# Edge rows of every third tile added on Pool instead of VectorE, in a graph-attention layer on one core

## The reference

```python
h = jnp.maximum(_layernorm(x, axis=-1), 0.0)          # x: 50000 x 256
msg = jax.nn.relu(h[src] + edge_attr)                 # 25000 edges, 256 wide
p = msg @ W_fc.T + b_fc
scores = p @ Q.T                                      # 4 heads
...
alpha = w / jnp.maximum(denom[dst], 1e-09)            # softmax over the edges of a node
pooled = segment_sum(alpha[:, h:h+1] * p, dst)        # for each head
gate = softmax(mean_p @ Wg.T + bg)                    # mean_p: mean of p over a node's edges
return x + sigmoid(einsum('nh,nht->nt', gate, pooled))
```

## Time and profile before

| | us |
|---|---|
| median of 3 runs | 658.44 |
| lowest, highest | 654.64, 659.47 |
| profiled execution, first to last instruction (the profile gives no other time of it) | 732.9 |
| VectorE busy in it | 487.6 |
| Pool busy in it | 453.4 |
| TensorE busy in it | 548.9 |

### The profile page before, as it was taken

The page is one execution under the profiler, slowest core; times in us unless marked ns, Lnnn a source line. Parts: engine busy times, 40 slices in busy tenths (PEclk is TensorE's granted clock), DMA queues, the critical chain, the costliest instruction groups (busy, mean ns, idle before and its releaser), DMA issues.

```text
span 732.9 us, 12416 instructions
## 1 busy us (share of the span) xinstructions
PE 548.9 (75%) x2474; PEld 434.1 (59%) x2475; DVE 487.6 (67%) x1644; ACT 383.3 (52%) x661; POOL 453.4 (62%) x339
## 2 busy tenths in 40 slices
PE   2417988878779868879403998888888778877785
PEld 2205876666558656758202876776667566665564
DVE  4208678788879768769798766666565655555555
ACT  2105455656457545647211254666666666666674
POOL 7765565665560656550053366777877887778785
PEclk9999899999999999989855999999999999999999
DMA  7434455555553468775300799999999999999999
GB/s 223 131 93 134 147 173 174 165 174 154 174 170 114 129 224 271 237 234 191 115 0 1 247 355 383 314 307 329 357 319 329 325 327 339 325 337 336 341 333 332
DMA packets 137238, 171.53 MB, mean 234 GB/s; under 512 B 10096, under 2 KB 123784, under 8 KB 137202
## 3 DMA queue, kind: packets, MB, share of 16 engines
q10 hardware_dynamic: 91344, 90.23, 37.6%
q1 hardware_dynamic: 33010, 42.70, 18.6%
q0 software_dynamic: 12848, 38.20, 16.5%
HBM read 111.50 MB, written 59.60 MB: 233 GB/s over the span
## 4 chain that ended last, share of the span: by engine, by line
PE 52%; issue 12%; ACT 11%; DVE 10%; another core or an unknown queue 5%; ACTq 4%; DVEq 3%; POOL 2%; DMA 2%; POOLq 0%; SPq 0%
PE bank L745 24%; PE bank L829 18%; PE bank L735 7%; ACT arena L597 5%; DVE spread L1248 3%; ACT bank L573 3%; POOL arena L478 2%; ACTq L600 2%; DVEq L1252 1%; ACT arena L505 1%; ACTq L552 1%; ACTq L605 1%; ACT arena L497 1%; DMA p_keep<-p_spill 1%
## 5 line engine op out<-in xcount | busy, mean ns | idle before, releaser
L829 PE MATMUL bank<-p_keep,spread 128*128 x1172 | 274.1, 388 | 51.6 <-DVE spread L1248 46.7
L829 PEld LDWEIGHTS bank<-p_keep,spread 128*128 128x128 f32 x1172 | 219.0, 192 | 107.5 <-issue 79.8
L1248 DVE TENSOR_SCALAR spread<-bank,rel,wgt 128x128 f32<-128x128 f32 x586 | 195.8, 404 | 128.5 <-PE bank L829 72.8
L478 POOL TENSOR_TENSOR arena<-arena 128x1024 f32<-128x1024 f32 x96 | 224.9, 2352 | 73.1 <-ACT arena L597 72.7
L745 PE MATMUL bank<-w_all,arena 128*128 128x264 f32 (+1 forms) x784 | 228.0, 417 | 53.2 <-ACT arena L505 40.2
L745 PEld LDWEIGHTS bank<-w_all,arena 128*128 128x128 f32 (+1 forms) x784 | 143.7, 204 | 78.9 <-ACT arena L505 50.9
L597 ACT ACTIVATE arena<-bank 128x1024 f32<-128x1024 f32 x97 | 99.2, 1023 | 139.3 <-PE bank L829 120.3
L443 POOL DMA_INDIRECT p_keep<-in_x_dram,idx x124 | 120.8, 975 | 72.6 <-issue 31.5
L505 ACT ACTIVATE arena<-bank 128x256 f32<-128x256 f32 x196 | 73.6, 376 | 124.2 <-PE bank L735 71.0
L443 POOL DMA_INDIRECT arena<-in_x_dram,idx x72 | 70.1, 973 | 64.7 <-ACT arena L497 33.7
L573 ACT ACTIVATE bank<-zero 128x1024 f32<-128x1024 f32 x98 | 100.5, 1026 | 3.0
(11 more groups left out here) (202 smaller groups left out, 190.6 us busy)
## 6 DMA issues: line engine op xcount, KB each, us to landing
out_dram<-arena ACTq DMA_DIRECT2D x97, 512.0 KB, 4.5
arena<-in_x_dram ACTq DMA_DIRECT2D x73, 512.0 KB, 5.4
arena<-in_edge_attr_dram SPq DMA_DIRECT2D x48, 512.0 KB
arena<-in_x_dram POOLq DMA_DIRECT2D x24, 512.0 KB, 5.8
p_spill<-p_keep SPq DMA_DIRECT2D x16, 512.0 KB
p_keep<-p_spill SPq DMA_DIRECT2D x16, 512.0 KB, 5.8
p_keep<-in_x_dram,idx POOLq DMA_INDIRECT x124
arena<-in_x_dram,idx POOLq DMA_INDIRECT x72
```

Source lines behind the costliest of these rows:

```text
L478: pool.tensor_tensor(yout[:, slot, :, :], yout[:, slot, :, :], xin[:, slot, :, :], ALU.add).then_inc(summed, 1)
L829: nc.tensor.matmul(places[:, bass.ds(place, T)], spread[:, k0 + k, :], p_rows[:, bass.ds(p_at, T)], start=False, stop=True, skip_group_che ...
L1248: v.tensor_scalar(spread[:, k, :], bank[:, 7, P:2 * P], rel[:, bass.ds(s0 + k, 1)], wgt[:, bass.ds(s0 + k, 1)], ALU.is_equal, ALU.mult).th ...
```

## The change

Of the tiles 18, 21, ..., 171 (52 of them) Pool adds the edge rows: tile `a` behind the gather of tile `a + 16`, once its edge rows are loaded and it is normalized. VectorE leaves these tiles out. A second semaphore, `added_by_pool`, counts Pool's adds, in the order of the tiles; who waited for `added` now waits for the share of each.

```diff
+    ADD_BEHIND = 16
...
+        def by_pool(t):
+            return 18 <= t < TILES - ADD_BEHIND - 8 and t % 3 == 0
+
+        POOL_BEFORE = [sum(by_pool(a) for a in range(n)) for n in range(TILES + 1)]
+
+        def wait_added(engine, n):
+            engine.wait_ge(added, n - POOL_BEFORE[n])
+            if POOL_BEFORE[n]:
+                engine.wait_ge(added_by_pool, POOL_BEFORE[n])
...
             def load_ea(quad):
                 if quad >= 4:
-                    sp.wait_ge(added, 4 * quad - BODY + 4)
+                    wait_added(sp, 4 * quad - BODY + 4)
...
                                         ).then_inc(gathered[k], 16)
+                a = t - ADD_BEHIND
+                if by_pool(a):
+                    q = (a // 4) % 4
+                    pool.wait_ge(ea_in[q], 16 * (a // BODY) + 16)
+                    pool.wait_ge(ln_done, a + 1)
+                    pool.tensor_tensor(u[:, a % 4, :], u[:, a % 4, :], ea[:, a % BODY, :], ALU.add
+                                       ).then_inc(added_by_pool, 1)
...
             def turn(t):
                 n = rows_of(t)
-                pe.wait_ge(added, t + 1)
+                if by_pool(t):
+                    pe.wait_ge(added_by_pool, POOL_BEFORE[t + 1])
+                else:
+                    pe.wait_ge(added, t + 1 - POOL_BEFORE[t + 1])
...
-                if 0 <= k - ADD_LAG < TILES:
+                if 0 <= k - ADD_LAG < TILES and not by_pool(k - ADD_LAG):
                     add_edge(k - ADD_LAG)
```

More of the change, by code:

```diff
@@ L275, in gnn_layer @@
         ea_in = [sem(f"ea_in{k}") for k in range(4)]
+        added_by_pool = sem("added_by_pool")
         stats_done, mv_done = sem("stats_done"), sem("mv_done")
```

## The result

The changed kernel takes 694.61 us (median of 4 runs, 688.31 to 698.45) against 656.54 for the kernel before on the same chip: a ratio of 1.0576, interval 1.0517 to 1.0634. That is 38 us slower; 693 was forecast.

What follows compares the result with a forecast made beforehand. Pool's gathers, one every 1.26 us, were taken to bound the loop. Floor 4.2 + 247 + 42.6 = 294, less 10, plus 33: 317 against 287, +30, plus 5 for stalls: 658.4 + 35, say 693 us; range 657 to 716, own range 670 to 712.

Steps and rivals of the forecast that it cites:

- Pool is the bound, and the 42.6 us lie on the path: Tiles 18 to 171: Pool needs 1.53 us a tile against 1.13 elsewhere, so its 52 adds lengthen the loop.
- The timed loop of before: Loop in the timed runs: 352.4 - 65 = 287 us, 15 us of stalls above the gathers' floor.
- The add: Each of 52 Pool adds behind a gather: 0.72 + 0.1 = 0.82 us, 42.6 us in all (31 to 70).
- The tail: Loop's end after Pool's last gather: 33 us against 30.6 behind the same gather before, 2 to 3 us more.
- Stalls: TensorE's leftover stalls in the loop, partly covered by Pool's longer rounds, partly on top: 5 us added.
- The step that failed: Loop: TensorE and VectorE each need about 1.13 us a tile, Pool's gathers at 1.26 are slowest.
- saves nothing by itself: Removing 52 of VectorE's adds, 21.2 us of busy time, gains no time because Pool is slower.
- Added waits at nothing: Pool's waits for edge rows and normalizing, TensorE's for Pool, and the extra semaphore waits in the loop: no cost.
- Contention at nothing: Pool adds may hold VectorE adds, 37 us at worst; VectorE has 62 us of room, so no cost.
- A: Rival: no cover or a dear add, each costs 1.35 us, 70 us in all, 720 us; chance 0.16.
- B: Rival: no change, Pool's idle time from TensorE's late releases takes the adds, 658 to 664 us; chance 0.12.
- C: Rival: faster, adds thin the dense gathers that cause late releases, 8 us saved, 650 us; chance 0.10.

Runs made afterwards that it cites:

- e1: Kernel before, VectorE still adding all tiles, plus 52 adds of 128x256 on scratch data on Pool: 683.62 us, ratio 1.0440 to before.
- e3: Kernel before with only the change's waits on Pool at the 52 places, no adds there: 657.38 us, ratio 0.9995 to before.
- e2: Changed kernel with every sixth tile added on Pool, 26 adds instead of 52: 678.93 us, ratio 1.0335 to before.
- e10: Kernel before plus a one-element-per-partition write on Pool behind each of 177 gathers: 658.18 us, ratio 1.0032 to before.
- e8: Changed kernel with Pool's add 10 tiles behind its gather instead of 16, same 52 tiles: 691.74 us, ratio 1.0516 to before.
- e5b: Kernel before with SP loading 29 tiles (37 to 121) as plain rows, not gathered by Pool: 652.43 us, ratio 0.9936 to before.
- e9: Changed kernel with the 52 adds made by nobody, those tiles left without edge rows: 655.30 us, ratio 0.9987 to before.
- e6b: Kernel before with 29 tiles loaded plain by SP, not gathered, and Pool adding edge rows of 29 tiles (21 to 105): 649.56 us, ratio 0.9895 to before.
- e4: Kernel before plus two 128x320 zero writes on Pool, reading nothing, at each of the 52 places: 702.48 us, ratio 1.0708 to before.
- e0: Kernel before, unchanged, run again for a trace of ordinary length (span 653.4 us): 655.52 us, ratio 0.9988 to before.

## Why the prediction was right, and where it was not

**Direction, size and cause hold.** The step "Pool is the bound, and the 42.6 us lie on the path" is what happened: Pool has hardly any idle time but the gaps, everyone waits for it, scratch adds alone cost 27 to 29 us (`e1`), the waits alone nothing (`e3`), and the longer queue goes with the number of adds, at 0.6 us each beside one wait (`e2`). The forecast of +35 stands against +38 in the time and +39.2 in the loop.

**Term by term,** two sizes were off and went against each other, and that 693 came out this near is luck.

- *The timed loop of before:* 287 in the prediction, 272.3 in the ordinary trace. That is the gathers' floor of 272 that stood in the prediction, by two differences that cancel: the last gather ends at 256.9, not 251.2, and the tail is 15.4, not 20.5. I had put 65 of the missing 74.5 us into the loop and 10 into the last stage; the loop had all of them (352.4 - 272.3 = 80). This put 15 us too little into the loss.
- *The add:* 0.82 (0.72 and a gap of 0.1), measured 0.67 on the queue: 34.6 us instead of 42.6, with the one wait of 3.8 in it. The add itself was well sized, with a median of 736 ns and a mean of 781. But it doesn't come on top of the gathers and their gaps: it starts 0.02 us behind a gather, in the gap that is there anyway, and the next gather follows it after 0.16 instead of 0.30. So in a clean round 4.41 - 3.78 = 0.63 of its 0.73 shows, and `e10` shows the gap by itself. The estimate of 0.56 worked out from the figure in the Trainium skill (GPSIMD Engine Reference, section 3.1) was too low: the shortest add takes 0.62 in `e1`, which reads one tile twice, and 0.73 in after.
- *The tail:* 2 to 3 forecast, 4.6 measured (20.0 against 15.4), and in the trace of `e8` it goes away with the lag. The 6 us that the prediction has in it for the last tile's way out came from no row.
- *Stalls:* +5 forecast. The mean round (4.53) is longer than a clean one (4.41), 51 x 0.12 = 6 us, but 3.8 of that is the one wait and 52 x 0.045 = 2.3 are adds longer than the median, and all of it is inside the 34.6.

From the true 272 the same steps would have given 317 + 5 - 272 = +50, or 708: further off than the two errors together left me. The upper end of the forecast's own range does not come out either: 693 and the 15 of its last term are 708, not 712.

**The step that failed:** "TensorE and VectorE each need about 1.13 us a tile, and Pool's gathers at 1.26 are the slowest of the three". VectorE needs 1.23 to 1.25 between tiles 50 and 100. Over the loop Pool and VectorE were tied, VectorE setting the pace between tiles 50 and 100 and Pool from 124 on: relief of either one gains next to nothing (`e5b` -0.6%, `e9` nothing), relief of both 1.05% (`e6b`), on 29 tiles. I had read the 17 us in which Pool paused as what every tile needs. It was one stretch, tiles 106 to 120, behind the last of VectorE's work on a table, which takes 0.14 us a tile between tiles 50 and 100; from 100 to 124 the ordinary trace of before needs 1.17. It did no harm here, because "saves nothing by itself" holds for another reason: Pool's queue ends at 256 to 257 in before and `e9` alike. Had Pool had some room, the step would have said "no gain" where `e6b` shows one.

**Added waits at nothing:** nearly right. Alone they cost nothing (`e3`); in after one of Pool's 52 waits for the normalizing lasted 3.8 us, and after's statistics wait 1.1 us for gathers in the whole loop. At a lag of 10 (`e8`) they wait 34, so the cover was thin but there.

**Contention at nothing:** nearly right for the time (the 2.3 us by which Pool's own adds are longer), wrong for the profile. I forecast 59 us for VectorE's 144 adds; they took 74.0. In VectorE's timeline of after one add stands beside Pool's add of 205.04:

```profile
204.23 0.40 DVE L1083 TENSOR_TENSOR arena<-arena 128x256 f32<-128x256 f32 x1
...
204.88 1.19 DVE L1083 TENSOR_TENSOR arena<-arena 128x256 f32<-128x256 f32 x1
```

1.19 us instead of 0.40, and it ends at 206.07, after Pool's add has ended at 205.77. `e4`, whose Pool operation reads nothing, leaves VectorE's adds at 407 ns. The Trainium skill (SBUF — State Buffer, "Who interferes with whom") says that a VectorE instruction with two SBUF inputs contends with a GpSimd instruction that reads SBUF, and not with one that only writes it. The traces agree, with 515 ns beside adds and 407 beside writes. VectorE had the time for it, since Pool set the pace.

**The rivals.** *A* (1.35 an add) fell with 0.67. *B* and *C* rested on TensorE's late releases being in the timed runs; `e0` shows that they are not, so Pool had no idle time to give. The view that would have said so was already there: a span 74.5 us above the median was evidence against reading its waits as the kernel's. *Against my signs:* I said that ScalarE's waits for TensorE would get shorter. They are 65.7 us, seven times those of an ordinary run of before, because they hand on TensorE's wait for Pool. And I said a tile every 1.5 us or more from 18 to 171: it is 1.51 by Pool's adds, (280.55 - 49.30) / 153, but 1.46 by TensorE's products.

**Open:** why that one execution was 75 us longer, with releases that came late. And no version that computes the layer and beats both kernels came out of this: one would need fewer or cheaper gathers on Pool, and none was tried.

## What to carry to other kernels

Before work is moved to another engine, work out that engine's queue as count times spacing, not as busy time: Pool's gathers were busy for 0.95 us and cost 1.26, and what is added to an in-order queue without idle time lengthens the kernel, here by some 0.6 us an add, however much the engine that gave it away is relieved. Then ask which engine is tied for the bound: relief of one of two alone shows as nothing, and that is not proof that it has room. And compare a trace's span with the timed runs first: waits in an execution that is 11% too long may be the execution's own.

## What the runs showed of the hardware that I had not expected

- The gap of 0.30 us between two gathers on Pool is partly free for another operation: 0.12 us in each gap leaves the gathers 1.26 apart (`e10`), and an add of 0.73 lengthens a round by 0.63.
- What an operation between two gathers costs is not its busy time: by the end of the queue, waits included, 0.81 us of writes cost 0.96 each time and 0.73 us of adding 0.67. The next gather starts 0.16 us behind an add, 0.36 behind the pair of writes, and 0.19 behind the small write of `e10`; what that gap depends on is not shown.
- An add on Pool and an add on VectorE lengthen each other: VectorE's from 407 to 515 ns in the mean, Pool's from 0.73, the shortest in after, to 0.78 in the mean and 1.06 for the longest; with writes alone on Pool VectorE's stay at 407.
